# Where the softmax's division is done: on the attention output by a broadcast matmul, or on the exponentials by GpSimd, in a re-ordered plan

## The reference, cut to what matters

```python
q = (rmsnorm(layernorm(x)) @ wq.T).reshape(B, L, NH, HD)
k, v = (memory @ wk.T).reshape(...), (memory @ wv.T).reshape(...)
attn = einsum('blhd,bmhd->bhlm', q, k) * HD ** -0.5
attn = where(mask, attn, -inf)
attn = nan_to_num(softmax(attn, axis=-1))
out = einsum('bhlm,bmhd->blhd', attn, v).reshape(B, L, C) @ wo.T
x = x + tanh(g_xattn[0]) * sigmoid(x @ wg.T) * out
# second layer, on the result
x_q = clip(round(xn / x_scale)); x = x + tanh(g_ffn[0]) * (x_q @ w_ternary * gamma * x_scale + bias)
```

## Time and profile before

| | us |
|---|---|
| median of 3 runs (range) | 1370.34 (1370.13 to 1373.58) |
| the profiled execution | 1371.29 |
| its span in the trace | 1369.6 |
| first `Sa` of groups 0, 1, 2, 3 | 39.30, 146.32, 250.89, 354.32 |
| end of the last `oP` of group 3 | 450.2 |
| start of layer 3 | 471.1 |
| TensorE busy over the span | 1230.6 (90%) |
| VectorE, ScalarE, GpSimd busy | 719.2, 553.2, 424.0 |

### The profile page before, as it was taken

How to read it: one execution, slowest core, us unless ns; L and a number is a source line. 1 busy time by engine, 2 the same in 40 slices (tenths; PEclk the granted TensorE clock), 3 DMA queues, 4 the chain that set the end, 5 groups by cost and what they waited for, 6 DMA issues and landing times. The chain is left out here.

```text
span 1369.6 us, 25480 instructions
## 1 busy us (share of the span) xinstructions
PE 1230.6 (90%) x7821; PEld 1034.4 (76%) x7822; DVE 719.2 (53%) x1443; ACT 553.2 (40%) x1430; POOL 424.0 (31%) x504
## 2 busy tenths in 40 slices
PE   6998999999997399969998998699999989999992
PEld 6876777777776177746776876699999878999992
DVE  5666655656645589953677643442334443424340
ACT  4543444444444188833121111543344443434341
POOL 1101211211211556540005721235444433444442
PEclk9999999999998699979999999899999999999997
DMA  9000000000000111143000204555446755545456
GB/s 326 25 16 19 17 1 18 17 1 17 1 2 1 33 45 38 38 141 118 0 1 0 94 31 137 159 129 100 77 80 141 195 142 116 132 86 135 86 140 169
DMA packets 53880, 103.62 MB, mean 76 GB/s; under 512 B 5126, under 2 KB 20998, under 8 KB 53750
## 3 DMA queue, kind: packets, MB, share of 16 engines
q1 hardware_dynamic: 38182, 65.78, 14.7%
q0 software_dynamic: 15632, 36.97, 14.3%
HBM read 75.99 MB, written 30.93 MB: 78 GB/s over the span
## 5 line engine op out<-in xcount | busy, mean ns | idle before, releaser
L1738 PE MATMUL t_H<-m_W,t_xT 128*128 128x352 f32 x1632 | 286.4, 332 | 16.7 <-DVE m_W L1816 13.9
L1738 PEld LDWEIGHTS t_H<-m_W,t_xT 128*128 128x128 f32 x1632 | 268.0, 193 | 18.7 <-DVE m_W L1816 14.8
L1705 POOL DMA_INDIRECT acc_d<-t_ys,t_sid x68 | 109.2, 1606 | 279.0 <-ACT t_ys L1767 191.5
L1783 ACT ACTIVATE t_sl<-t_H 128x352 f32<-128x352 f32 x68 | 31.5, 463 | 175.4 <-PE t_H L1738 173.7
L597 ACT ACTIVATE pr<-pr 128x128 f32<-128x128 f32 x256 | 76.0, 298 | 55.2 <-DVE pr L758 53.9
L62 PE MATMUL t_Y<-m_W,t_hT 128*128 128x512 f32 (+1 forms) x207 | 88.2, 426 | 9.4 <-DVE t_hT L1861 6.4
L1837 DVE TENSOR_TENSOR t_h<-t_H,t_sl 128x352 f32<-128x352 f32 x68 | 35.5, 523 | 106.5 <-ACT t_sl L1783 106.5
L1767 ACT ACTIVATE t_ys<-t_Y,t_wcol 128x512 f32<-128x512 f32 x69 | 47.3, 685 | 94.8 <-PE t_Y L64 94.8
L1859 DVE TENSOR_TENSOR t_hT<-t_TH,t_hT 128x256 fp32r<-128x256 f32 x68 | 28.7, 422 | 107.1 <-ACT t_hT L1804 105.9
L64 PE MATMUL t_Y<-m_W,t_hT 128*128 128x512 f32 (+1 forms) x207 | 82.3, 397 | 0.0
L63 PE MATMUL t_Y<-m_W,t_hT 128*128 128x512 f32 (+1 forms) x207 | 82.0, 396 | 0.0
(11 more groups left out here) (415 smaller groups left out, 3229.6 us busy)
## 6 DMA issues: line engine op xcount, KB each, us to landing
m_r<-in_L_ffn_w_dram SPq DMA_DIRECT2D x26, 704.0 KB, 5.1
m_r<-in_L_ffn_w_dram SPq DMA_DIRECT2D x13, 512.0 KB, 3.9
aCX<-in_ctx_dram SPq DMA_DIRECT2D x20, 256.0 KB, 2.6
rows_d<-before_w SPq DMA_DIRECT2D x17, 256.0 KB, 2.0
CT<-in_ctx_dram SPq DMA_DIRECT2D x8, 512.0 KB, 3.8
X<-in_x_dram SPq DMA_DIRECT2D x4, 1024.0 KB, 13.0
acc_d<-X SPq DMA_DIRECT2D x4, 1024.0 KB, 4.2
m_r<-in_L_ffn_sw_dram SPq DMA_DIRECT2D x4, 704.0 KB, 5.4
```

Source lines behind the costliest of these rows:

```text
L1705: pool.indirect_dma_start(out=m["acc_d"][:, :], out_offset=bass.IndirectOffsetOnAxis(ap=sid[:, b:b + 1], axis=0), in_=ys[:, b, :], in_offs ...
L1738: x_ = pe.matmul(bk[b % 2][:, 0:I], xT[:, b % 2, jx, k, :], W13[:, jw, k, j, :], start=k == 0 and jx == jw, stop=k == KC - 1 and jx == 1)
```

## The change

The division moves in front of the transpose. `sm` on VectorE now takes the maximum and then one small instruction that makes -scale times the maximum (`neg`, 128 x 4); the exponentials read the scores in PSUM with `neg` as their bias, so that SC comes free with the exponentials and not with the subtraction. A new step `nr.t` for each bank: VectorE takes the larger of each sum and 0.5 and its reciprocal (two instructions of 128 x 4), and GpSimd multiplies the 128 x 512 exponentials by it. `pT.t` waits for that. The steps `rc`, `bc` and `on`, the tile `o` and the bank REC are gone; O has two banks, and `oT` splits O directly. The list of a group is written anew, with `pv`, `pT`, `uT` and `fm` between projections.

```diff
-                f"Sa.0 xT.2 Sb.0 sm.0 sm.1 v.0 st.-2 st.-1 cT.2 ra.-1 xT.3 {d[0]} g.0 rb.-1 pT.0 cT.3 q.1.0 rd.-1 Sa.1 pT.1 Sb.1 "
...
+                f"Sa.0 xT.2 Sb.0 sm.0 sm.1 v.0 st.-2 st.-1 nr.0 cT.2 nr.1 ra.-1 xT.3 {d[0]} g.0 rb.-1 pT.0 rd.-1 q.1.0 "
+                f"Sa.1 pT.1 Sb.1 sm.2 sm.3 mk.4 q.1.1 sf.-4 sf.-3 cT.3 q.1.2 nr.2 pv.0 u.-2 {d[1]} nr.3 q.1.3 uT.-2 pT.2 u.-1 {d[2]} k.1.0 "
...
+                f"Sa.5 pT.9 Sb.5 sm.10 sm.11 mk.6 q.2.0 st.0 cT.5 q.2.1 nr.10 pv.4 q.2.2 nr.11 pT.10 {d[7]} q.2.3 "
...
                     elif kind == "sm":
                         act.wait_ge(s_out, 2 * t + 2)
+                        wait(act, t_fill, at(T_KINDS, ("pT", t - 2)))
                         for slot in range(HQ):
-                            pp, at_ = pr[:, t % 2, slot, :], t % HQ * HQ + slot
-                            i = act.activation(pp, pp, ACT.Exp, scale=SCALE0, accum_out=sums[:, t // HQ % 2, at_:at_ + 1])
+                            i = act.activation(pr[:, t % 2, slot, :], SC[t % 2][:, slot * S:(slot + 1) * S], ACT.Exp, scale=SCALE0,
+                                               bias=neg[:, t % 2, slot:slot + 1], accum_out=sums[:, t % 2, slot:slot + 1])
                         i.then_inc(p_exp, 1)
-                    elif kind == "bc":
-                        act.wait_ge(pv, at(PV, s))
-                        wait(act, o_lo, t)
-                        act.activation(o[:, :], REC[:, :], ACT.Copy).then_inc(r_out, 1)
...
+                    elif kind == "nr":
+                        pp = pr[:, t % 2, :, :]
+                        pool.wait_ge(inverse, 2 * t + 2)
+                        pool.tensor_tensor(pp, pp, rec[:, t % 2, :].unsqueeze(2).to_broadcast([P, HQ, S]), ALU.mult)\
+                            .then_inc(p_norm, 1)
...
-                            pe.wait_ge(p_exp, t + 1)
+                            pe.wait_ge(p_norm, t + 1)
...
-                        dve.tensor_tensor(pr[:, t % 2, :, :], bk, mx[:, t % 2, :].unsqueeze(2).to_broadcast([P, HQ, S]),
-                                          ALU.subtract).then_inc(s_out, 1)
-                    elif kind == "rc":
-                        dve.wait_ge(p_exp, HQ * t + HQ)
-                        wait(dve, pv, at(PV, ("bc", t - 2)))
-                        dve.reciprocal(rec[:, t % 2, :], sums[:, t % 2, :]).then_inc(o_norm, 1)
-                    elif kind == "on":
-                        dve.wait_ge(pv, at(PV, ("pv", 2 * t + 1)))
-                        dve.wait_ge(r_out, t + 1)
-                        dve.tensor_tensor(o[:, :], O[:, :], o[:, :], ALU.mult).then_inc(o_norm, 1)
+                        wait(dve, p_exp, t - 1)
+                        dve.tensor_scalar(neg[:, t % 2, :], mx[:, t % 2, :], MASKED / 10, -SCALE0, ALU.max, ALU.mult).then_inc(s_out, 1)
+                    elif kind == "nr":
+                        dve.wait_ge(p_exp, t + 1)
+                        wait(dve, p_norm, t - 1)
+                        dve.tensor_scalar(some[:, t % 2, :], sums[:, t % 2, :], 0.5, None, ALU.max).then_inc(inverse, 1)
+                        dve.wait_ge(inverse, 2 * t + 1)
+                        dve.reciprocal(rec[:, t % 2, :], some[:, t % 2, :]).then_inc(inverse, 1)
```

More of the change, by code:

```diff
@@ L185, in attention_heads_and_ternary @@
         T, M, SC = bank("T", 2), bank("M", 2), bank("SC", 2)
-        O, REC = bank("O", 1)[0], bank("REC", 1)[0]
+        O = bank("O", 2)
         mask_f = dg[0:NB, :]
@@ L221, in steps @@
                         continue
-                elif kind in ("sm", "pT"):
+                elif kind in ("sm", "nr", "pT"):
                     nums[0] += NQ * g
@@ L259, in attention_heads_and_ternary @@
         M_KINDS, X_UPD, STATS = BY_ACT + BY_DVE, ("oP", "fm"), ("sx", "st", "sf")
-        PV = ("pv", "bc")
         order = {}
@@ L290, in attention_heads_and_ternary @@
         s_half, s_fill, s_out, p_exp, pv = (sem(n) for n in ("s_half", "s_fill", "s_out", "p_exp", "pv"))
-        o_norm, r_out, o_hi, o_lo = (sem(n) for n in ("o_norm", "r_out", "o_hi", "o_lo"))
+        inverse, p_norm, o_hi, o_lo = (sem(n) for n in ("inverse", "p_norm", "o_hi", "o_lo"))
         added, biased, q_step, f_step = (sem(n) for n in ("added", "biased", "q_step", "f_step"))
         U_STEPS, F_STEPS = 6, 8
[L294 to L302, removed]
+        RING = SC + O
         with nc.Block() as block:
@@ L503, in _ @@
                                 pe.wait_ge(w_lo, KC * len(ORDER))
-                            wait(pe, s_out, 4 * t)
+                            wait(pe, p_exp, 2 * t)
                             if half == 0:
@@ L525, in _ @@
                             pe.wait_ge(m_dve, at(BY_DVE, ("v", b)))
-                            wait(pe, o_norm, 2 * b)
+                            wait(pe, o_lo, b - 1)
                         for jj in range(2):
@@ L529, in _ @@
                             for r in range(HQ):
-                                i = pe.matmul(O[r * HD:(r + 1) * HD, j * S:(j + 1) * S], va[:, j * HQ + r, :],
+                                i = pe.matmul(O[b % 2][r * HD:(r + 1) * HD, j * S:(j + 1) * S], va[:, j * HQ + r, :],
                                               pT[:, r % 2, r // 2 * 2 + jj, :], start=True, stop=True)
-                        i.then_inc(pv, 1)
-                    elif kind == "bc":
[L534 to L538, removed]
-                                i = pe.matmul(REC[r * HD:(r + 1) * HD, j * S:(j + 1) * S],
-                                              rec[:, t % 2, at_:at_ + 1].to_broadcast([P, HD]), identF[:, :],
-                                              start=True, stop=True)
                         i.then_inc(pv, 1)
```

38 lines of the change are left out of this document (16 added, 22 removed).

## The result

The changed kernel took 1397.71 us in the median (1395.09 to 1400.39, 4 runs) against 1370.24 of the kernel before (1367.04 to 1373.58, 4 runs): ratio 1.0193, 95% interval 1.0168 to 1.0219. Its profiled execution has a span of 1394.6 us, 25.0 longer than before; from the first `Sa` to the first transpose of layer 3 it needs 458.0 us against 434.3 (39.30 to 473.59), and the rest of the kernel is as long as it was, to about 1 us.

A forecast was written before the change was run, and what follows sets the result against it. TensorE's own list was taken to bound the kernel. Longer-chain waits less the `bc` saving gave +13.6 us, +17 with the clock, so 1388 from 1371.3; forecast 1386 us, own range 1378 to 1394, 8 in 10 1371 to 1399.

The forecast's parts named there:

- The sign: Whole kernel: chances were slower 0.76, within 0.3% 0.13, faster 0.11.
- rival (b): Waits as forecast, and the clock stays low after more of them or the port bites: 1394 to 1401 us; chance 0.20.
- +0.3 for the clock: Phase 1, the 2.45 us wait at `uT.-2`: might lower TensorE's clock, put at 1 us in all.
- +8.85: A middle group: new TensorE waits summed over the phases, 8.85 us, less 3.55 for `bc`, giving +5.3.
- The terms of group 0: Group 0: waits of 9.7 less 3.55 for `bc`, about +6, less 4 for waits already there: +2 us.
- The spreading steps: TensorE's `bc`, 16 times at 0.89 us: 14.2 us removed, the whole gain on the bounding engine.
- The chain behind a score pair: From scores to transpose: four exponentials take 1.6 us, GpSimd's product 1.27; transposes possible at F + 4.5 and F + 6.1.
- The row with a column as scale: ScalarE copy, 685 ns against 594 without: taken as the exponentials' bias price, 0.09 us each.
- Places: Waits by phase in a middle group: 0.6, 1.9, 1.0, 0.2, 2.0, 0.3 and, at the group's end, 2.85 us.
- The step that failed: group 3: Last group: about +1 us, since earlier waits at its end go and give most of its losses back.
- their followers: End of group 3: waits following the 4.3 us for exponentials, also expected to go; no separate size given.
- The shared port: VectorE quantisings beside GpSimd: if 12 on the path stretch by 0.4 us each, +5 us, 1391.

The follow-up runs named there:

- e4: The changed kernel with idle 512-column matmuls added ahead of three waits (12 before `uT.0`, 8 before `uT.-2`, 7 before `q.1.0`): 1386.29 us, ratio 1.0115.
- e1: The kernel before with each of the sixteen spreading matmuls `bc` executed twice: 1379.38 us, ratio 1.0062.
- e8: The changed kernel's division with the old list, long ready projections moved ahead of transposes that waited, `xT.3` ahead of `ra.-1`: 1344.73 us, ratio 0.9811.
- e10: e8 with `nr.1` directly behind `xT.3` and `fm.0` between `pT.15` and `pv.7`: 1337.44 us, ratio 0.9770.
- e9: The kernel before, its old division kept, with the same moves of TensorE's steps as e8: 1358.58 us, ratio 0.9926.
- e5: The changed kernel with the product by the reciprocals on VectorE instead of GpSimd: 1396.10 us, ratio 1.0171.
- e3: The changed kernel with `u.0` put ahead of `oP.2` in the list: 1393.90 us, ratio 1.0166.

## Why the prediction was right, and where it was not

The direction and the mechanism held: in-order queues turned the longer chain behind the scores into waits worth more than `bc`. The sign was 76% sure. The time came out 12 us above the forecast of 1386: outside that forecast's own range (1378 to 1394), inside the one of rival (b), where the clock stays low after more of the waits, and only 1 us inside the range for 8 in 10. Groups 0 to 2 lasted as long as was forecast (107 to 112 us); group 3, for which 96 to 99 stood, lasted 108.2.

**A middle group, taken apart.** The two windows at clock 1.00 give the busy time of TensorE without stretches at the lower clock: 96.65 us with `bc`, 93.13 without. Before, group 1 was 99.70 busy and 4.90 idle; the changed one is 97.95 busy and 11.35 idle. So: `bc` -3.5, stretches at the lower clock 3.05 to 4.8 or +1.8, idle time +6.4, sum +4.7. Group 2 in the same way: -3.5, +3.0, +6.4, sum +5.9. The prediction had -3.55, +0.3 for the clock (1 us in all for phase 1, over three groups) and +8.85. Its +5.3 and a little was right by luck, because two errors cancelled. The waits were too long: `pT.4` was to wait 1.0 and TensorE to be idle 1.5 before `uT.1`, and neither came. The clock was too cheap: it fell behind `q.1.0` and `uT.-2` too (the three windows of e4 above), where the sum had next to nothing. In group 0 the clock cost 2.5 us, as the sum had it, but the waits grew by 2.5 only, where 9.7 less 4 stood, so that groups 0 to 2 together grew by 12.0 where 15.6 was forecast. (The terms of group 0 add up to 9.95, not 9.7.)

**The spreading steps**, 14.2 us: right as their length and as the term of a sum in which the waits and the clock stand apart, which is how it was used. But it would have been wrong as a gain by itself: adding them once more cost 6 to 9 us in the old list (e1), and only lists with few waits show the whole (e8 and e10 against e9).

**The chain behind a score pair.** The first bank's four exponentials take 1.38 us, between the 1.26 and 1.6 that were weighed, and the product 1.04, not 1.27. The changed kernel's ScalarE in group 1, first, second and fifth exponential of the pair:

```profile
225.67 0.37 ACT L582 ACTIVATE pr<-SC,neg 128x128 f32<-128x128 f32 x1 [0.97 <-DVE neg L738]
...
226.03 0.36 ACT L582 ACTIVATE pr<-SC,neg 128x128 f32<-128x128 f32 x1
...
227.05 0.38 ACT L582 ACTIVATE pr<-SC,neg 128x128 f32<-128x128 f32 x1
```

The row with a column as scale was near in kind, but the bias cost a third of that price here (0.34 us from start to start against 0.31 before, not 0.40).

**Places.** `uT.0`: 3.20 measured, 3.3 forecast, for the reason given. Phase 1, `uT.-2`: 2.15 against 2.45. `q.1.0`: 1.94 against 1.1; here two held instructions (below) stand ahead of it in VectorE's queue. That they are the reason is argued, not tested: with the two products in their place (e5) it waited 2.04. `oP.3`: 0.90 against 1.35. `uT.1` did not wait; from `uT.0` to it went 3.51 us against 3.05, with 0.42 idle and the steps between at the lower clock. Waits for `fu` 20.8 us in eight cases, where 25 in eleven stood; for the product 14.3, where 12 stood. GpSimd was busy for 35.5 us, not 38.

**The step that failed: group 3.** It had +1 by "the waits of its end before go, which gives most of its losses back", and for the clock +0.3 as the middle groups; it grew by 12.2. The sum as it stands leaves +3.0 once the 4.3 us for exponentials are off; the other 2 are "their followers", which no row priced. The waits of before did go, but 3.46 us at `pT.10` (for which 4 was forecast), 2.19 at `pT.13` (in the sum nothing stood there) and 3.20 at `uT.0` took their place [the rows of group 3 above]. The larger part is the clock: with e10's group 3 (81.4 us busy at 0.98) as measure and 3.5 more for `bc`, the lower clock cost 1.3 us before (86.3 busy up to 450.36) and 10.9 after (92.3). That is +9.6 from the clock, +6.1 idle and -3.5, together +12.2. Windows of the changed kernel's group 3 show where (the clock is the number ahead of the last two):

```profile
420.00:435.00 15.00, 11.67 (x92) 8.63 (x90) 6.58 (x18) 7.99 (x36) 4.37 (x4) 1.00 0.01 2
435.00:447.00 12.00, 11.82 (x65) 8.97 (x66) 2.91 (x9) 4.10 (x18) 2.11 (x3) 0.72 0.00 0
447.00:460.00 13.00, 8.10 (x56) 5.78 (x55) 7.67 (x28) 5.08 (x20) 4.97 (x5) 0.86 0.00 1
460.00:473.50 13.50, 10.97 (x46) 7.04 (x48) 6.04 (x12) 2.99 (x5) 6.04 (x5) 0.50 0.00 1
```

The first long wait ends at 435.18 and is followed by 0.72; after the last, at 460.54, the engine stands at its lower level, 0.50, until 473.3, in the middle of the last `oP`, with further waits of 0.41, 0.90 and 0.69 us on the way. A sum that puts one fixed price of 2.4 us behind a group misses that. By the traces this group is 11 us above the forecast, and the groups before it 3.6 below.

**The shared port** was taken for a stretch of 0.4 us at the quantisings of 512 columns. In the changed kernel 7 of the 16 first scalings (L634) were stretched, six to 0.73 to 0.88 us and one, in group 3, to 1.65, against 0.55; no second one (L641) was. All seven are of the second tile of a pair, for which TensorE hardly waited, but for the 0.90 us before `uT.1` in group 3. So the price was near nothing on this path; in e3 and e5 scalings were stretched for which TensorE waited, by 1.5 us (e3, group 1) and 0.8 (e5).

## What to carry to other kernels

When a step is removed from the bounding engine at the price of a longer chain elsewhere, that engine's new waits take the gain (in the old list 8.9 us of idle time against 14.2 of work, and the median stood still), and it comes back only when the list is rewritten so that long independent work lies ahead of each late operand. When a division of work makes a chain longer, read the waits of a build in the old order and move one cover to each; done place by place from the trace it gave 26 to 33 us here, while a wholesale new order lost 27. Look at the last iteration separately: work for the next one, used as cover, is not there, and several waits close together cost more by the clock than by themselves (9.6 against 6.1 us in group 3).

## What the runs showed of the hardware

**VectorE is held, not slowed, while GpSimd works.** VectorE and GpSimd of the changed kernel in phase 0 of group 2:

```profile
264.81 1.04 POOL L377 TENSOR_TENSOR pr<-pr,rec 128x512 f32<-128x512 f32 x1 [5.26 <-DVE rec L744]
265.22 0.65 DVE L742 TENSOR_SCALAR some<-sums 128x4 f32<-128x4 f32 x1
...
266.17 1.04 POOL L377 TENSOR_TENSOR pr<-pr,rec 128x512 f32<-128x512 f32 x1 [0.32 <-DVE rec L744]
266.31 0.92 DVE L605 TENSOR_SCALAR mean<-mean 128x2 f32<-128x2 f32 x1
```

265.22 + 0.65 = 265.87 and 266.31 + 0.92 = 267.23; the products end at 265.85 and 267.21. These small instructions take 0.15 to 0.17 us alone and end with GpSimd's. A scaling of 512 columns ends 0.28 us behind it: in e3 L634 at 246.89 and L641 at 249.29, GpSimd's adds at 246.61 and 249.00. With the product on VectorE no small one is held (e5), but its L636 is, 1.29 us beside an add. Not every kind is held: in e3, between 246.56 and 249.0, the reduction L637 took 0.69 and the steps of one column, L638 and L639, 0.15 us with GpSimd busy beside them, as long as ever. The Trainium skill (SBUF — State Buffer, Who interferes with whom) says that the pair of ports shared by the two engines is an exclusive lock, for VectorE instructions with two SBUF inputs and for scalings that can use both ports, and that reductions never meet it. The trace agrees with all of these: a product of two inputs, L624, took 0.99 us beside GpSimd (at 239.12, 0.16 in e5), and the scalings and the reduction stand above. For a forecast it means: count a hold of up to the length of GpSimd's instruction at each small VectorE step beside it, and ask whether somebody waits for that step: in e3 `uT.1` did, in e5 `uT.0`, and in the changed kernel, so far as the order of the queue tells, `q.1.0`.

**Idle matmuls can pay.** With 27 more matmuls a middle group, e4 was 11 us faster than the changed kernel, since the clock stayed at its upper level (1.00 in the groups 0 to 2). They are a remedy for an order that waits, not better than one that doesn't: e10 is 49 us faster than e4.

**The same wait doesn't always cost the same clock.** TensorE waited 2.77 us before `uT.0` in groups 0, 1 and 2 of the kernel before, and the three groups show 1.00, 0.97 and 0.98; behind the wait of group 1 a matmul of 512 columns took 0.63 us instead of 0.39 (e1, at 238.51). In the changed kernel waits of 1.94 and 2.15 us were enough (the three windows of e4).
